# A decoder layer with 64 experts: slot table from running token counts in place of scatters

## The reference

```python
x = layernorm(x + self_attention(x))            # 16 heads of 16, rotary
x = layernorm(x + cross_attention(x, context))  # 120 keys, two softmaxes, difference weighted by lambda
x = layernorm(x + ffn(x))
```

```python
scores = sigmoid(x @ router_weight.T)
top_idx = top_k(scores + expert_bias, 6)
probs = top_scores / (sum(top_scores) + 1e-20)
pos = rank of the token among all tokens that chose this expert, in token order
valid = pos < CAP
y = gelu(xs @ w1[e]) @ w2[e]      # xs: up to CAP rows of expert e
out[token] += y * prob            # valid pairs only
shared = gelu(x @ sw1.T) @ sw2.T
return out + shared
```

## Time and profile before

| what | value |
|---|---|
| median of 3 runs | 2068.88 us |
| lowest, highest | 2061.9, 2072.28 us |
| profiled execution, own time | 2057.82 us |
| its span | 2056.0 us |
| mean granted TensorE clock | 0.915 of full speed |
| TensorE busy | 1719.1 us (84%), 14560 matmuls |
| VectorE busy | 1269.6 us (62%) |
| ScalarE busy | 1086.8 us (53%) |
| POOL busy | 1275.7 us (62%), 1303 instructions |
| DMA | 300.94 MB, mean 146 GB/s |

### The profile page before, as it was taken

The page is one execution under the profiler, slowest core; times in us unless marked ns, Lnnn a source line. Parts: engine busy times, 40 slices in busy tenths (PEclk is TensorE's granted clock), DMA queues, the critical chain, the costliest instruction groups (busy, mean ns, idle before and its releaser), DMA issues. The chain is left out here.

```text
span 2056.0 us, 45046 instructions
## 1 busy us (share of the span) xinstructions
PE 1719.1 (84%) x14560; PEld 1200.8 (58%) x14560; DVE 1269.6 (62%) x2887; ACT 1086.8 (53%) x1701; POOL 1275.7 (62%) x1303
## 2 busy tenths in 40 slices
PE   3799999999999877988888888888887724999985
PEld 2566666666676654555555555555554413888874
DVE  3567676766767756777777777777777421232265
ACT  1466666666666655666656666666665400111134
POOL 4567676776767422366666666666665573677576
PEclk7899999999999998998988899999998656999998
DMA  4676877778778665665645556655554104778687
GB/s 119 145 193 166 197 182 188 190 172 195 179 189 185 171 135 127 117 119 120 120 101 109 103 103 114 118 118 112 107 108 79 31 25 142 189 187 204 151 284 263
DMA packets 322362, 300.94 MB, mean 146 GB/s; under 512 B 80626, under 2 KB 299572, under 8 KB 313040
## 3 DMA queue, kind: packets, MB, share of 16 engines
q1 hardware_dynamic: 299728, 286.56, 58.8%
q0 software_dynamic: 22528, 13.03, 4.1%
HBM read 187.28 MB, written 111.17 MB: 145 GB/s over the span
## 5 line engine op out<-in xcount | busy, mean ns | idle before, releaser
L1704 POOL DMA_INDIRECT slot_table<-att_cross_tok_i,att_cross_slot_i x384 | 382.3, 996 | 142.4 <-issue 106.3
L1344 DVE TENSOR_REDUCE att_nmax<-self_p_mx 128x2 f32<-128x512 f32 x512 | 329.1, 687 | 202.1 <-PE self_p_mx L628 201.7
L1434 DVE TENSOR_REDUCE att_cross_nmax<-self_p_mx 128x8 f32<-128x960 f32 x256 | 294.9, 1152 | 148.0 <-PE self_p_mx L828 111.4
L1079 ACT ACTIVATE att_probs<-self_p_sc 128x1024 f32<-128x1024 f32 x256 | 261.3, 1021 | 93.8 <-PE self_p_sc L616 91.6
L1172 ACT ACTIVATE att_probs<-self_p_sc 120x1024 f32<-120x1024 f32 x256 | 261.7, 1022 | 77.1 <-PE self_p_sc L810 45.2
L628 PE MATMUL self_p_mx<-att_k_stack,att_q_stack 96*128 96x256 bf16 x1024 | 161.1, 277 | 58.2 <-DMA att_k_stack<-self_k_parts 52.9
L828 PE MATMUL self_p_mx<-att_k_stack,att_q_stack 48*128 48x120 bf16 x2048 | 108.7, 228 | 116.0 <-DVE att_cross_nmax L1434 58.4
L846 PE MATMUL self_p_pv<-att_probs,att_v_aug 120*32 120x256 f32 x2048 | 184.4, 431 | 3.6 <-issue 2.3
L828 PEld LDWEIGHTS self_p_mx<-att_k_stack,att_q_stack 48*128 48x128 bf16 x2048 | 71.9, 101 | 165.9 <-DVE att_cross_nmax L1434 85.4
L616 PE MATMUL self_p_sc<-att_q_stack,att_k_stack 99*128 99x256 bf16 x1024 | 158.5, 278 | 10.0 <-ACT att_probs L1079 10.0
L1980 PE MATMUL ffn_ph<-ffn_xT,ffn_sw 128*128 128x256 f32 x512 | 118.3, 385 | 48.1 <-DMA ffn_x_sb<-x_and_gates 48.1
(11 more groups left out here) (174 smaller groups left out, 3614.4 us busy)
## 6 DMA issues: line engine op xcount, KB each, us to landing
att_q_stack<-self_q_parts SPq DMA_DIRECT2D x64, 256.0 KB, 5.6
expert_sums<-att_zeros SPq DMA_DIRECT2D x64, 256.0 KB
att_q_stack<-cross_q_parts SPq DMA_DIRECT2D x128, 128.0 KB
ffn_w<-in_ffn_w SPq DMA_DIRECT2D x64, 256.0 KB
ffn_m_sb<-expert_sums SPq DMA_DIRECT2D x32, 512.0 KB, 5.4
self_q_parts<-att_parts SPq DMA_DIRECT2D x32, 384.0 KB, 2.8
self_k_parts<-att_parts SPq DMA_DIRECT2D x32, 384.0 KB, 3.8
att_k_stack<-self_k_parts SPq DMA_DIRECT2D x32, 384.0 KB, 7.8
```

Of the source, the lines that this page charges most:

```text
L1079: act.activation(probs[:, g % 4, :], p_sc[:, :, :].rearrange("p b n -> p (b n)"), ACT.Exp, scale=SCALE).then_inc(s_exp, 1)
L1344: dve.tensor_reduce(nmax[:, M.slot, :, m], p_mx[:, m % 2, :].rearrange("p (c k) -> p c k", c=TC), AX_X, ALU.max, negate=True).then_inc(s_r ...
L1434: dve.tensor_reduce(cnmax[:, M.slot, :, :, 2 * m:2 * m + 2].rearrange("p c e h -> p e h c"), p_mx[:, :, 0:4 * KEYS].rearrange("p e (x k) - ...
L1704: pool.indirect_dma_start(out=table[:, :], out_offset=bass.IndirectOffsetOnAxis(ap=slot_i[:, Q.slot, tc, k:k + 1], axis=0), in_=tok_i[:, Q ...
```

## The change

The scatters, the sort of the slots and the running mask sum go away. In the cross stage, each batch's mask is multiplied (as the stationary side) with a triangle of ones, which gives for each expert and token t the number of tokens up to t in this batch that chose the expert. VectorE copies these 64 x 256 counts to bf16 and SyncE stores them in DRAM.

At the front of the experts' stage the counts of all batches are loaded, a partition per batch and group of 16 experts. A matmul with a block triangle gives the first slot of each batch; comparisons with the slot numbers 0 to 95 mark which batch a slot is in; 64 small matmuls with the marks turn this into facts of each slot. Per pair of experts, a matmul with the marks then fetches for each slot the counts of its batch, and VectorE counts how many of them are at most the number left: that is the token's place, and with the batch's first token the token number. POOL waits for each pair's numbers before it gathers. The schedule of the stage is moved: the first gather stands at unit 4, transposes follow 3 units after the gather and not 4, and the finish is spaced by 5/4 of a unit.

```diff
# attention, sync: store of the counts; the table's clearing (L492, L493) is gone
                 if Q.on:
                     sp.wait_ge(c_prob, Q.n + 1)
                     sp.dma_start(cy_rows[Q.n][:, :, DM:DM + N_EXP], prob[:, Q.slot, :, :]).then_inc(c_pst[Q.slot], 16)
+                    sp.wait_ge(c_cnt, Q.n + 1)
+                    sp.dma_start(counts_out[Q.n], counts[:, Q.slot, :]).then_inc(c_cst[Q.slot], 16)
# attention, tensor
                     pe.wait_ge(c_mask, R.n + 1)
-                    if past(R.n, 1):
-                        pe.wait_ge(c_msum, 2 * R.n)
-                    for tc in range(TC):
-                        out = p_k[:, tc * N_EXP:(tc + 1) * N_EXP]
-                        pe.matmul(out, earlier[:, :], mask[:, tc, :], start=True, stop=False)
-                        if tc == 1:
-                            pe.matmul(out, everyone[:, :], mask[:, 0, :], start=False, stop=False)
-                        pe.matmul(out, everyone[:, :], mask_sum[:, :], start=False, stop=False)
-                        mm = pe.matmul(out, ones[:, :], e_number[:, :], start=False, stop=True)
+                    pe.matmul(p_k[0:N_EXP, 0:P], mask[:, 0, :], until[:, :], start=True, stop=True)
+                    pe.matmul(p_k[0:N_EXP, P:T], mask[:, 0, :], ones[:, :], start=True, stop=False)
+                    mm = pe.matmul(p_k[0:N_EXP, P:T], mask[:, 1, :], until[:, :], start=False, stop=True)
                     mm.then_inc(c_pos, 1)
# attention, vector: positions (L1508) becomes copy_counts; sort_slots (L1514) and its call are gone
+            def copy_counts(R):
                 dve.wait_ge(c_pos, R.n + 1)
-                dve.tensor_tensor(key[:, :, :], p_k[:, 0:TC * N_EXP].rearrange("p (c e) -> p c e", c=TC),
-                                  mask[:, :, :], ALU.mult).then_inc(c_key, 1)
+                if past(R.n, 3):
+                    dve.wait_ge(c_cst[R.slot], 16 * R.turn)
+                dve.tensor_copy(counts[:, R.slot, :], p_k[0:N_EXP, 0:T]).then_inc(c_cnt, 1)
# attention, gpsimd: scatter, scatter_in_round (L1701 to L1715), all their calls, the token numbers
# (L1728, L1735), the mask sums (L1777 to L1783) and the last wait (L1788, L1789) are gone
```

```diff
# feed_forward
+    GROUPS = P // n_batches
+    OF_GROUP = N_EXP // GROUPS
+    N_COUNTS = GROUPS + 2
+    PREFIX, META = 1, 3
-    GATHER = [k * 9 // 8 for k in range(N_PAIRS)]
+    GATHER = [k * 9 // 8 + 4 for k in range(N_PAIRS)]
+    SLOTS = [max(META, k + 1) for k in range(N_PAIRS)]
-    FINISH = [LAST_Y + 1 - (NF - 1 - f) * 4 // 3 for f in range(NF)]
+    FINISH = [LAST_Y + 1 - (NF - 1 - f) * 5 // 4 for f in range(NF)]
-    turn_at = {u + 4: k for k, u in enumerate(GATHER)}
-    hidden_at = {u + 5: k for k, u in enumerate(GATHER)}
-    out_at = {u + 6: k for k, u in enumerate(GATHER)}
-    add_at = {u + 7: k for k, u in enumerate(GATHER)}
+    slots_at = {u: [k for k in range(N_PAIRS) if SLOTS[k] == u] for u in set(SLOTS)}
+    turn_at = {u + 3: k for k, u in enumerate(GATHER)}
+    hidden_at = {u + 4: k for k, u in enumerate(GATHER)}
+    out_at = {u + 5: k for k, u in enumerate(GATHER)}
+    add_at = {u + 6: k for k, u in enumerate(GATHER)}
# sync
-            sp.dma_start(slots[:, :], table.rearrange("(c e) o -> c (e o)", e=N_EXP)).then_inc(s_tb, 16)
             for u in range(-4, END):
+                if u == -3:
+                    sp.dma_start(steps[:, :], C["steps"]).then_inc(s_cl, 16)
+                    sp.dma_start(blocks[:, :], C["blocks"]).then_inc(s_cl, 16)
+                    for g in range(GROUPS):
+                        sp.dma_start(count[g * n_batches:(g + 1) * n_batches, :, :],
+                                     counts[:, g * OF_GROUP:(g + 1) * OF_GROUP, :]).then_inc(s_cl, 16)
# tensor, at the end of a unit
+                if u == PREFIX:
+                    pe.wait_ge(s_cl, 16 * N_COUNTS)
+                    pe.wait_ge(s_cc, 1)
+                    pe.matmul(p_ye[:, 0:OF_GROUP], blocks[:, :], own_n[:, :], start=True, stop=True).then_inc(s_pre, 1)
+                if u == META:
+                    pe.wait_ge(s_cc, 9)
+                    for g in range(GROUPS):
+                        if g:
+                            pe.wait_ge(s_meta, g)
+                        of = slice(g * n_batches, (g + 1) * n_batches)
+                        for j in range(OF_GROUP):
+                            at = 64 + 3 * (g * OF_GROUP + j)
+                            mm = pe.matmul(p_ye[0:CAP, at:at + 3], in_batch[of, j, :], facts[of, j, :],
+                                           start=True, stop=True)
+                        mm.then_inc(s_meta, 1)
+                for k in slots_at.get(u, ()):
+                    if k >= 2:
+                        pe.wait_ge(s_sf, k - 1)
+                    for j in range(EJ):
+                        e = k * EJ + j
+                        g, x = e // OF_GROUP * n_batches, e % OF_GROUP
+                        mm = pe.matmul(p_cnt[0:CAP, k % 2, j * T:(j + 1) * T], in_batch[g:g + n_batches, x, :],
+                                       count[g:g + n_batches, x, :], start=True, stop=True)
+                    mm.then_inc(s_cp, 1)
# vector, after L2055; at u == PREFIX: own_n from the counts' last column, the facts, the first slots from
# PSUM, then from_first, from_beyond and in_batch over [128, 16 x 96]
+                if u == META:
+                    fact = p_ye[0:CAP, 64:64 + 3 * N_EXP].rearrange("p (e m) -> p e m", m=3)
+                    dve.wait_ge(s_meta, GROUPS)
+                    dve.tensor_scalar(left[:, :], fact[:, :, 0], -1.0, steps[0:CAP, CAP + 1:CAP + 2], ALU.mult, ALU.add)\
+                       .then_inc(s_bc, 1)
...
+                for k in slots_at.get(u, ()):
+                    dve.wait_ge(s_cp, k + 1)
+                    for j in range(EJ):
+                        e = k * EJ + j
+                        ins = dve.tensor_scalar(at_most[:, e % (2 * EJ), :], p_cnt[0:CAP, k % 2, j * T:(j + 1) * T],
+                                                left[:, e:e + 1], base[:, e:e + 1], ALU.is_le, ALU.add,
+                                                accum_out=slots_f[:, e:e + 1])
+                    ins.then_inc(s_sf, 1)
+                    dve.wait_ge(s_sf, k + 1)
+                    dve.tensor_copy(slots[:, k * EJ:(k + 1) * EJ], slots_f[:, k * EJ:(k + 1) * EJ]).then_inc(s_sl, 1)
# gpsimd, before each gather
-            pool.wait_ge(s_tb, 16)
+                    pool.wait_ge(s_sl, k + 1)
```

More of the change, by code:

```diff
@@ L99, in run_both, with attention @@
         whole(cross_step(lambda lag, t=t: At(t, t, lag, n_batches, shift)))
-def attention(nc, n_batches, x_in, xT_in, W, ctxT_in, CW, consts, y_out, res_out, z_out, yT_out, table, moe):
+def attention(nc, n_batches, x_in, xT_in, W, ctxT_in, CW, consts, y_out, res_out, z_out, yT_out, counts_out, moe):
     LAGS = 6
@@ L449, in cross_loads @@
                          (w_r[:, :, :], CW["r"].rearrange("(f p) e -> p f e", p=P)),
-                         (earlier_f[:, :], consts["earlier"])]
+                         (until_f[:, :], consts["until"])]
                 loads += [(lam_in[:, n, :], CW["lam"][n:n + 1, :].to_broadcast([P, 8])) for n in range(4)]
@@ L600, in _ @@
                 sp.wait_ge(c_tst[p], 16 * len(range((p - n_batches) % 3, n_batches, 3)))
+                sp.wait_ge(c_cst[p], 16 * len(range((p - n_batches) % 3, n_batches, 3)))
         @block.tensor
@@ L1699, in step @@
                         .then_inc(s_lo, 1)
-            def scatter(Q, at):
-                for x in at:
-                    tc, k = x // TOP, x % TOP
-                    pool.indirect_dma_start(
-                        out=table[:, :], out_offset=bass.IndirectOffsetOnAxis(
-                            ap=slot_i[:, Q.slot, tc, k:k + 1], axis=0),
-                        in_=tok_i[:, Q.slot, tc:tc + 1], in_offset=None, bounds_check=N_EXP * CAP - 1,
-                        oob_is_err=False).then_inc(c_scat[Q.slot], 16)
@@ L1746, in cross_step @@
+            def cross_step(at_lag):
+                A, O = (at_lag(lag) for lag in (1, 5))
                 if A.on:
@@ L1793, in attention, with feed_forward @@
     nc.all_engine_barrier()
-def feed_forward(nc, outer, n_batches, W, C, x2, x2T, table, moe, out):
+def feed_forward(nc, outer, n_batches, W, C, x2, x2T, counts, moe, out):
     n_tok = n_batches * T
@@ L1842, in feed_forward @@
         slots = sb("slots", [CAP, N_EXP], I32)
+        steps = sb("steps", [P, CAP + 4])
+        blocks = sb("blocks", [P, P])
+        count = sb("counts", [P, OF_GROUP, T], BF16)
+        own_n = sb("own_counts", [P, OF_GROUP])
+        first = sb("first_slots", [P, OF_GROUP])
+        beyond = sb("slots_beyond", [P, OF_GROUP])
+        from_first = sb("from_first", [P, OF_GROUP, CAP], BF16)
+        from_beyond = sb("from_beyond", [P, OF_GROUP, CAP], BF16)
+        in_batch = sb("in_batch", [P, OF_GROUP, CAP], BF16)
+        facts = sb("batch_facts", [P, OF_GROUP, 3], BF16)
```

(18 more changed lines are left out.)

168 lines of the change are left out of this document (54 added, 114 removed).

## The result

The changed kernel takes **1955.7 us** (median of 4 runs, 1943.7 to 1964.2) against 2070.6 (4 runs, 2061.9 to 2072.5): ratio 0.944, 95% interval 0.9412 to 0.9469. The forecast was 2044, range 2018 to 2064. It missed, by 88 us on the fast side.

What follows compares the result with a forecast made beforehand. It took TensorE, busy 84% of the span, as the bound, with scatters setting the cross stage's end. Terms -31 - 8 + 13 + 3 - 1.5 = -24.5 us, from the median 2068.9, gave 2044, range 2018 to 2064.

Steps and rivals of the forecast that it cites:

- Inside the cross loop POOL's scatters hold nobody: Cross loop: no engine waits for the scatters, so removing them gains nothing there by itself.
- term of 8 us: Cross loop: 8 us gained, two thirds of 25 x 0.47 = 12, bounds 0 and 12.
- 0.47 us of sort ahead of L1447: Cross loop: VectorE loses 0.47 us a batch of sorting ahead of the normalisation for which TensorE waits.
- The stacks, for which I allowed up to 10 us: Cross loop: stacks come 0.4 us a batch later; slack covers it, otherwise 26 x 0.4 = 10 us lost.
- Rival B: Cross loop: the clock stops falling, 37 us gained in place of 8, whole 2015; chance 0.13.
- Stage end: End of the cross stage: the scatters set it; without them the next stage starts 31 us earlier, 28 to 35.
- Experts' front: Front of the experts' stage: added loads, prefix, small matmuls and counting cost 13 us, bounds 8 and 20.
- Middle: Middle of the experts' stage: two more matmuls a pair cost 3 us, partly taken up by lag, bounds 1 and 6.
- rival D: Experts' middle: VectorE's counting falls into the ring of adds, 36 us over 32 pairs, whole 2080, slower; chance 0.06.
- End: End of the experts' stage: one token tile already loaded, 1.5 us gained, bounds -4 and 0; closer finish under same traffic.
- My own sign of a wrong forecast: Experts' stage: span from first transfer to the end growing by over 30 us would show the forecast wrong.
- rival C: Cross loop gives nothing and the experts' front costs 20 us: whole 2059, or about 2052 with one only; chance 0.20.

Runs made afterwards that it cites:

- short runs: Groups of runs in which the kernel before, without any edit, took 1933 to 1959 us.
- no_scatters: The kernel before without its scatters and all waits for them, slot sort and POOL's other steps kept: 23.29 us a batch.
- earlier_front: The changed kernel with small matmuls and gathers one unit earlier and the finish again 4/3 of a unit apart: 1942.2 us, ratio 0.9985 to the kernel before.
- the first and the second group of experiments: Two sets of four kernels, without scatters or with added work or writes; the kernel before beside them took 2060.2 us in the first, 1958.6 in the second.
- long groups: Groups of runs in which the kernel before, without any edit, took 2058 to 2078 us.
- before_padded: The kernel before with three more internal DRAM tensors of 384 KB each, 96 KB of each written once early: 1944.8 us, ratio 0.9991.

## Why the prediction was wrong

**Cross loop: the step that failed.** "Inside the cross loop POOL's scatters hold nobody" was read from the waits between named instructions, and was false in the runs forecast: about 3.2 us a batch went where TensorE's results were done and VectorE and ScalarE started 1 to 2 us late. The term of 8 us was right neither there (98.6) nor in short runs (0.3 the other way). Only taking the scatters away, with the sort kept, gives it back (23.29), and POOL work in their place doesn't bring it on (23.02). What I had priced, 0.47 us of sort ahead of L1447, is worth nothing: with the sort and without scatters the loop is as fast as the changed kernel's. The stacks, for which I allowed up to 10 us, are now waited for longer (13 times and 17.0 us at L813, 3.8 before), and the loop is faster all the same. Rival B isn't it: a batch at the full clock took 25.9, and 23.5 is below that; the mean granted clock, 860 to 1530 us, went from 0.91 to 0.94 only.

**Stage end: right in kind, 38.3 for 31.** The gates are ready 14.4 us after the start of the last residual sum (1576.99 + 0.42 against 1563.0), as forecast. The 11.7 us gap from the earlier trace rows that I kept whole is 4.0 behind the last store; the other 7.7 went with the scatters. I had the case that the stores land faster, but with 35 as the bound, and 38.3 is outside. That it is the scatters and not the sort shows in no_scatters, whose stage change takes 20.1 us.

**Experts' front: +17.1 for +13**, inside 8 to 20. TensorE in the changed kernel, and the first steps of VectorE:

```profile
1595.56 0.17 DVE L2012 CAST ffn_own_counts<-ffn_counts 128x16 f32<-128x16 bf16 x1 [9.12 <-DMA ffn_counts<-token_counts]
...
1600.21 0.96 DVE L2027 TENSOR_TENSOR ffn_in_batch<-ffn_from_first,ffn_from_beyond 128x1536 bf16<-128x1536 bf16 x1
```

```profile
1604.01 3.55 PE L1935 MATMUL ffn_p<-ffn_batch_facts,ffn_in_batch 32*96 32x3 bf16 x61
...
1609.62 0.66 PE L1944 MATMUL ffn_pcnt<-ffn_counts,ffn_in_batch 32*96 32x256 bf16 x2 [1.60 <-DVE ffn_at_most L2043]
1610.21 6.32 PE L1901 MATMUL ffn_p<-ffn_sw,ffn_hT 128*128 128x256 f32 x16
1616.46 0.41 PE L1944 MATMUL ffn_pcnt<-ffn_counts,ffn_in_batch 32*96 32x256 bf16 x2
1616.81 3.72 PE L1910 MATMUL ffn_ph<-ffn_xT,ffn_sw 128*128 128x256 f32 x16
...
1625.21 0.55 PE L1880 MATMUL ffn_p<-ffn_ident,ffn_xg 96*128 96x96 f32 x4
```

The counts landed at start + 13.3 (forecast 12) and the prefix was done at + 18.9 (forecast 19). The 64 small matmuls took 3.5 us where I had 1.9 from the row: 3.55 us for 61 is 0.058 each, at a granted clock of 1.00 (1604 to 1608), and the row had 0.03. For the isolated matmul of up to 64 columns the Trainium skill (TensorE: Matmul & The Clock Gate, Back-to-back issue gap) gives about 60 cycles at 2.4 GHz, 25 ns, and says that this is too little for a stream with a weight load before each matmul. The trace agrees, with its 58 ns; the seven of the row, each with a weight load too, went at 0.03, and why is not shown. The unit behind them (L1901 at 1610.21) took 6.32 us for 3.65, 2.7 us that I had only in the bound. It runs near the 1.2 GHz level, behind the small matmuls and the 1.6 us wait for VectorE; windows of the changed kernel:

```profile
1605.00:1610.00 5.00, 3.28 (x54) 2.70 (x54) 2.16 (x9) 0.00 (x0) 0.00 (x0) 0.87 0.22 56
1610.00:1616.50 6.50, 6.50 (x19) 4.83 (x17) 2.00 (x10) 0.00 (x0) 4.43 (x5) 0.58 0.20 58
```

**Middle: +5.9 for +3**, inside 1 to 6. From 1743.2 to the last add at 1945.35 it was 202.2, now 208.0, with TensorE busy in all of it. A pair's two counting matmuls take 0.35 us (1616.46 to 1616.81, and as long at the full clock: 1629.17 to 1629.52), not 0.2. VectorE's counts are covered, as said, and rival D did not come: the last add starts 8.9 us behind its matmul, where it was 10.9:

```profile
1828.58 1.03 PE L1920 MATMUL ffn_p<-ffn_w,ffn_heT 128*96 128x256 f32 x4
```

The accumulator shows as a second instruction of 0.08 us and costs nothing here. That there are two is what the Trainium skill (VectorE: DVE Perf Modes, Two Vector instructions with no wait between them) says, and the trace agrees:

```profile
1609.02 0.54 DVE L2043 TENSOR_SCALAR_CACHE_REDUCE ffn_at_most<-ffn_pcnt,ffn_slots_left,ffn_first_tokens 96x256 bf16<-96x256 f32 x1
1609.49 0.08 DVE L2043 DVE_READ_ACCUMULATOR ffn_at_most<-ffn_pcnt,ffn_slots_left,ffn_first_tokens 96x1 f32 x1
```

**End: +8.7 for -1.5**, outside my -4 to 0. I called the closer finish (5/4) free "under the same traffic". SyncE's queue in the changed kernel:

```profile
1858.68 0.50 SPq L1841 DMA_DIRECT2D ffn_xT<-x_by_feature  x1
1861.81 0.37 SPq L1844 DMA_DIRECT2D ffn_x_sb<-x_and_gates  x1
1862.81 0.92 SPq L1860 DMA_DIRECT2D ffn_m_sb<-expert_sums  x2
1863.78 0.51 SPq L1864 DMA_DIRECT2D out<-ffn_o_sb  x1
1870.25 0.92 SPq L1860 DMA_DIRECT2D ffn_m_sb<-expert_sums  x2
1871.21 0.51 SPq L1864 DMA_DIRECT2D out<-ffn_o_sb  x1
1871.76 0.50 SPq L1841 DMA_DIRECT2D ffn_xT<-x_by_feature  x1
```

Between two tiles' loads (L1841) stand two finishes, each with a wait of SyncE, and the next tile's load goes out 13.1 us after the last; in the kernel before these loads (L1911, 1949 to 1984 us) go out 7.5 to 10.5 us apart. From the last add on, traffic fell from 270 to 246 GB/s and the granted clock from 0.92 to 0.84 (before, the same columns):

```profile
1945.35:2056.00 110.65, 78.33 (x343) 64.90 (x341) 61.12 (x155) 44.31 (x86) 75.32 (x81) 0.92 0.83 270
```

With 4/3 again (earlier_front) 5.1 of the 8.7 us come back. That edit moved the front too, so the spacing as the cause is likely and not shown; the rest is open.

**Together.** Without the loop my terms were -31 + 13 + 3 - 1.5 = -16.5; measured -38.3 + 17.1 + 5.9 + 8.7 = -6.6. In the runs forecast the loop's 98.6 hid that, so that the change came out faster was luck: nearly all of the gain came from where I had said that the scatters hold nobody. My own sign of a wrong forecast came as well: from its first transfer the stage grew by over 30 us (31.7), through a slow front and the end, not through D. Where the kernel before is short there is nothing to hide it: stage change -38.3, experts' stage +36.5, and the change is worth nothing, 1.0034, interval 0.9993 to 1.0075. That is near rival C.

**What stays open.** Why the same code is 110 us longer in some groups. It isn't the chip alone: the first and the second group of experiments ran on the same one, 21 minutes apart. The three groups in which it was short each began with a kernel that holds 1.2 MB more internal memory in DRAM; the three in which it was long (the comparison of the two kernels among them) held none such. That is no proof, and something that changes from one time to another would fit as well; two placements beside each other in one group, one long and one short, would be. Nor is it shown whether a dear word is dear by its address, its size or its being a packet, as no spread or wide scatter met a long group; nor by what way the scatters hold the engines.

## What to carry to other kernels

Look at what the waits of a kernel are put down to, and take "remote" ones as seriously as named ones: engines that start 1 to 2 us after their input is done are a cost of its own, and here nearly the whole gain lay there. Before believing a gain of a few per cent from taking tiny transfers away, time both kernels in several groups of runs: its scatters of single words cost this kernel nothing in one and 3 to 4 us a batch in another. And small work is priced by rows of its own kind: a matmul of three columns by one of three columns, a queue of finishes by what stands between two loads.

## What was not expected of the hardware

- In long groups 1536 single words a batch, by POOL's scatters (38.8 and 35.7 us a batch) or by one plain transfer of SyncE (33.6), brought "remote" waits where the changed kernel (23.0 to 23.5) has none. In one place of the latter ScalarE and VectorE stood still for 6 us and TensorE for 3 of them, in the middle of a group without waits. In short groups the same number of scattered rows cost 0.1 to 0.6 us a batch above 22.9.
- The page counts 12288 packets for the 384 scatters (22528 in the queue, 10240 without them), 32 for one of 128 rows.
- Scatters whose rows are all out of bounds are counted with as many packets as others, and cost 5.8 us a batch in a long group.
- The queue of the scatters showed nothing of it: its packets took 4.1% of 2056 us in the kernel before, long, and 4.3% of 1937 in before_padded, short, about 84 us both times.
